# LayerNorm row sums: from f32 matmuls on x to bf16 matmuls on a copy written by ScalarE

## Chip, cores and metric

The kernel runs on the 8 cores of one Trainium2 chip, with the same program and different data on each core. The metric is the device time of the slowest core in microseconds (us).

## What is computed

One "macaron" layer on x of shape 2 x 4096 x 2048 in f32: half a feed-forward block, attention, half a feed-forward block, each on a LayerNorm of x.

```python
def _layernorm(x, axis=-1, eps=1e-5):
    m = jnp.mean(x, axis=axis, keepdims=True)
    v = jnp.var(x, axis=axis, keepdims=True)
    return (x - m) / jnp.sqrt(v + eps)
...
    x = x + 0.5 * _L0_ffn_ref(_layernorm(x, axis=-1), L0_ffn_U, L0_ffn_V, L0_ffn_W1, L0_ffn_b1, L0_ffn_W2, L0_ffn_b2)
    x = x + _L0_attn_ref(_layernorm(x, axis=-1), L0_attn_Wq, L0_attn_Wk, L0_attn_Wv, L0_attn_q_to_latent, L0_attn_v_up, L0_attn_Wo)
    x = x + 0.5 * _L0_ffn_ref(_layernorm(x, axis=-1), L0_ffn_U, L0_ffn_V, L0_ffn_W1, L0_ffn_b1, L0_ffn_W2, L0_ffn_b2)
```

The feed-forward block is a mixture over 8 low-rank maps (V, then U) with weights softmax(relu(x W1) W2). The attention is causal with 16 heads and 64-wide latent keys and values.

## The kernel before

Each core owns 1024 tokens of one sequence, but computes keys and values for all 4096 of it, in four blocks of 1024 tokens. The activations lie transposed: `x_res` is 128 partitions x 16 chunks x 1024 tokens in f32, where chunk c holds features 128c to 128c+127. A sum over the features of a token is therefore a sum over partitions and chunks, and TensorE makes it with a column of ones as weights, accumulating over the chunks in PSUM.

For each of the four blocks (loop `for j in range(4)`, from line 754) the order is:

1. Four loads of `x_res` (L762), issued by the sync engine. From the second block on, each waits until the previous block's second LayerNorm has read its chunks.
2. `emit_ln` (LN1) writes the scaled activations to `xhat` in bf16.
3. `emit_ffn`: the dense projection with W1 (`emit_big_proj`, L320), the mixture weights, the product with V (L517), their gate, replicated by two small matmuls for each of four parts (L547) and multiplied in by VectorE (L557), the product with U (L575), and the addition to `x_res` on VectorE (L585).
4. `emit_ln` again (LN2), into the same `xhat`.
5. The key/value projection (L787), which reads `xhat`; VectorE copies the result out (L805), and its TensorE token is `kv_tok`.

Behind the fourth block come the query projection, the attention, the output projection (additions to `x_res` in L1563), a ninth `emit_ln` into `xhat3`, a last feed-forward block and the store.

So `emit_ln` runs nine times. In it, a sum stage loops over the 16 chunks. ScalarE (ACT) squares the chunk into the bf16 buffer `ln_sq` (L178). TensorE makes four matmuls of 512 columns: two f32 ones straight from `x_res` into `ln_sum` (L185, L188), then, after waiting for the square, two bf16 ones from the square into `ln_sq` in PSUM (L192, L194). There is one square buffer (the list of two names the same one twice), so ACT waits with each square for TensorE's last matmul of the chunk before. Then VectorE and ACT work out mean and reciprocal deviation (L201 to L226), TensorE replicates it over the partitions (L232, L234), and VectorE multiplies all 16 chunks into `dst` (L244), which is `xhat`.

At the end of `emit_ln` and of `emit_ffn` a `load_fence` makes TensorE and ACT wait for VectorE's last product or addition, so that neither starts the next stage early. `wait0` hands `emit_ln` one token for each chunk: a load's in LN1, an addition's in the others. All order between engines is in semaphores written by hand: `ct` counts TensorE, `cs` ACT, `cv` VectorE.

Of the kernel before, what the change touches and what calls it, by code (L numbers as in the profile page):

```python
# [12 lines left out]
AF = mybir.ActivationFunctionType  # L13
# [5 lines left out]
NTOK = 1024  # L19
# [11 lines left out]
def uid():  # L31
    _UID[0] += 1
    return _UID[0]
# [102 lines left out]
def load_fence(block, engines, sem, val):  # L136
    for name in engines:
        @getattr(block, name)
        def _(e):
            e.wait_ge(sem, val)  # L140
# [12 lines left out]
def emit_ln(nc, block, bufs, S, src_chunks, dst, wait0=None, mrr=None):  # L153
    w0 = wait0 if isinstance(wait0, list) else \
        ([wait0] + [None] * (NCH - 1) if wait0 is not None else [None] * NCH)
    ct, cs, cv = S['ct'], S['cs'], S['cv']
    onesb = bufs['ones_bf']
    u = uid()
    with contextlib.ExitStack() as ps:
        p_sum = ps.enter_context(nc.psum_tensor(f"ln_sum{u}", [1, NTOK], F32))  # L160
        p_sq = ps.enter_context(nc.psum_tensor(f"ln_sq{u}", [1, NTOK], F32))
        p_rrep = ps.enter_context(nc.psum_tensor(f"ln_rrep{u}", [128, NTOK], F32))
        sq2 = [ps.enter_context(nc.sbuf_tensor(f"ln_sq2_{u}0", [128, NTOK],
                                               BF16))] * 2
        m_sb = ps.enter_context(nc.sbuf_tensor(f"ln_m{u}", [1, NTOK], F32))
        t2 = ps.enter_context(nc.sbuf_tensor(f"ln_t2{u}", [1, NTOK], F32))
        rstd = ps.enter_context(nc.sbuf_tensor(f"ln_r{u}", [1, NTOK], F32))
        sq_toks = []
        mm_toks = []
        for c in range(NCH):  # L170
            par = c % 2
            @block.scalar
            def _(s, c=c, par=par):
                if w0[c] is not None:
                    s.wait_ge(w0[c][0], w0[c][1])
                if c >= 1:
                    s.wait_ge(ct.h, mm_toks[c - 1])
                s.activation(sq2[par][:, :], src_chunks[c],  # L178
                             AF.Square).then_inc(cs.h, 1)
            sq_toks.append(cs.inc())  # L180
            @block.tensor
            def _(t, c=c, par=par):
                if w0[c] is not None:
                    t.wait_ge(w0[c][0], w0[c][1])
                t.matmul(p_sum[:, 0:512], bufs['ones_f'][:, 0:1],  # L185
                         src_chunks[c][:, 0:512],
                         start=(c == 0), stop=(c == NCH - 1))
                t.matmul(p_sum[:, 512:1024], bufs['ones_f'][:, 0:1],  # L188
                         src_chunks[c][:, 512:1024],
                         start=(c == 0), stop=(c == NCH - 1))  # L190
                t.wait_ge(cs.h, sq_toks[c])
                t.matmul(p_sq[:, 0:512], onesb[:, 0:1], sq2[par][:, 0:512],  # L192
                         start=(c == 0), stop=(c == NCH - 1))
                t.matmul(p_sq[:, 512:1024], onesb[:, 0:1],  # L194
                         sq2[par][:, 512:1024],
                         start=(c == 0), stop=(c == NCH - 1)).then_inc(ct.h, 1)
            mm_toks.append(ct.inc())
        @block.vector
        def _(v):
            v.wait_ge(ct.h, mm_toks[-1])  # L200
            v.tensor_scalar(m_sb[:, :], p_sum[:, :], 1.0 / E,  # L201
                            None, ALU.mult).then_inc(cv.h, 1)
            v.wait_ge(cv.h, cv.n + 1)
            v.tensor_tensor(t2[:, :], m_sb[:, :], m_sb[:, :],
                            ALU.mult).then_inc(cv.h, 1)
            v.wait_ge(cv.h, cv.n + 2)
            v.tensor_scalar(t2[:, :], t2[:, :], EPS, None,
                            ALU.subtract).then_inc(cv.h, 1)
            v.wait_ge(cv.h, cv.n + 3)
            v.scalar_tensor_tensor(t2[:, :], p_sq[:, :], 1.0 / E, t2[:, :],  # L210
                                   ALU.mult, ALU.subtract).then_inc(cv.h, 1)
        cv.inc(3)
        var_tok = cv.inc()
        @block.scalar
        def _(s):
            s.wait_ge(cv.h, var_tok)
            s.activation(rstd[:, :], t2[:, :], AF.Ln).then_inc(cs.h, 1)
            s.wait_ge(cs.h, cs.n + 1)
            s.activation(t2[:, :], rstd[:, :], AF.Exp,
                         scale=-0.5).then_inc(cs.h, 1)  # L220
        cs.inc(1)
        rstd_tok = cs.inc()
        @block.vector
        def _(v):
            v.wait_ge(cs.h, rstd_tok)
            v.scalar_tensor_tensor(mrr[:, :], m_sb[:, :], -1.0, t2[:, :],  # L226
                                   ALU.mult, ALU.mult).then_inc(cv.h, 1)
        mr_tok = cv.inc()
        @block.tensor
        def _(t):  # L230
            t.wait_ge(cs.h, rstd_tok)
            t.matmul(p_rrep[:, 0:512], bufs['onesr_f'][:, :], t2[:, 0:512],  # L232
                     start=True, stop=True)
            t.matmul(p_rrep[:, 512:1024], bufs['onesr_f'][:, :],  # L234
                     t2[:, 512:1024], start=True, stop=True).then_inc(ct.h, 1)
        rep_tok = ct.inc()
        last = None
        apply_toks = []
        for c in range(NCH):
            @block.vector  # L240
            def _(v, c=c):
                if c == 0:
                    v.wait_ge(ct.h, rep_tok)
                v.tensor_mul(dst[:, NTOK * c:NTOK * (c + 1)], src_chunks[c],  # L244
                             p_rrep[:, :]).then_inc(cv.h, 1)
            last = cv.inc()
            apply_toks.append(last)
        load_fence(block, ('tensor', 'scalar'), cv.h, last)
        return last, apply_toks, mr_tok
# [342 lines left out]
def alloc_common(nc, e):  # L592
    b = {}
    b['w2_sb'] = e(nc.sbuf_tensor("w2_sb", [128, NCH * 8], BF16))
    b['b1_sb'] = e(nc.sbuf_tensor("b1_sb", [128, NCH], F32))
    b['b2_sb'] = e(nc.sbuf_tensor("b2_sb", [8, 1], F32))
    b['repsel_sb'] = e(nc.sbuf_tensor("repsel_sb", [8, 4 * 128], BF16))
    b['ident_f'] = e(nc.sbuf_tensor("ident_f", [128, 128], F32))
    b['ident_bf'] = e(nc.sbuf_tensor("ident_bf", [128, 128], BF16))
    b['ones_f'] = e(nc.sbuf_tensor("ones_f", [128, 1], F32))  # L600
    b['ones_bf'] = e(nc.sbuf_tensor("ones_bf", [128, 1], BF16))
    b['onesr_f'] = e(nc.sbuf_tensor("onesr_f", [1, 128], F32))
    b['onesr_bf'] = e(nc.sbuf_tensor("onesr_bf", [1, 128], BF16))
    b['consts'] = e(nc.sbuf_tensor("consts_sb", [1, 2], F32))
    return b
# [33 lines left out]
def build_fused():  # L639
# [38 lines left out]
    with contextlib.ExitStack() as stx:  # L678
# [5 lines left out]
        bufs = alloc_common(nc, e)  # L684
# [6 lines left out]
        ct, cs, cv = S['ct'], S['cs'], S['cv']  # L691
# [7 lines left out]
        with contextlib.ExitStack() as ph1:  # L699
# [50 lines left out]
            for j in range(4):  # L750
                xq_toks = []
                for qd in range(4):
# [5 lines left out]
                    def _(sy, j=j, qd=qd, rel=rel, dxn=dx.n):  # L758
                        sy.wait_ge(dx.h, dxn)
                        if rel is not None:  # L760
# [5 lines left out]
                    xq_toks.append(dx.inc(16))  # L766
                w0 = [(dx.h, xq_toks[c // 4]) for c in range(NCH)]
                _, ln1_ap, mr1 = emit_ln(nc, block, bufs, S, x_chunks, xhat,
                                         wait0=w0, mrr=mrr1)
                res_toks = emit_ffn(nc, block, bufs, S, x_chunks, xhat,  # L770
# [3 lines left out]
                                    first=(j == 0), zps=kv_ps)  # L774
                w2l = [(cv.h, res_toks[c]) for c in range(NCH)]
                _, ln2_q, mr2 = emit_ln(nc, block, bufs, S, x_chunks, xhat,
                                        wait0=w2l, mrr=mrr2)
                if True:
# [21 lines left out]
                    kv_tok = ct.inc()  # L800
# [9 lines left out]
                def _(g, j=j, kvs_tok=kvs_tok):  # L810
# [3 lines left out]
                    g.dma_start(out=vt512[:, :, 128 * j:128 * j + 128],  # L814
                                in_=kv512[64:128, :, :]).then_inc(dlat.h, 16)
                dlat.inc(32)

            def qt_cb(m, pap, mm_tok):
                @block.vector
                def _(v, m=m, pap=pap, mm_tok=mm_tok):  # L820
                    v.wait_ge(ct.h, mm_tok)
                    v.tensor_copy(bbuf[:, NTOK * m:NTOK * (m + 1)],
                                  pap[:, :]).then_inc(cv.h, 1)
                return (cv.h, cv.inc())
# [720 lines left out]
        with contextlib.ExitStack() as f2:  # L1545
# [13 lines left out]
            def wo_cb(m, pap, mm_tok):  # L1559
# [12 lines left out]
            zps2 = f2.enter_context(  # L1572
                nc.psum_tensor("zps2", [128, NTOK], F32))
            _, ln3_ap, mr3 = emit_ln(
                nc, block, bufs, S, x_chunks, xhat3,
                wait0=[(cv.h, wo_toks[c]) for c in range(NCH)], mrr=mrr3)
# [98 lines left out]
```

## Time and profile before

| | |
|---|---|
| median of 3 runs | 3349.59 us (3349.21 to 3351.09) |
| the profiled execution | 3348.29 us |
| its span, slowest core (core 4) | 3346.8 us |
| spans of all cores | 3331.1 to 3346.8 us |
| mean granted TensorE clock | 0.743 to 0.745 on all cores |
| busy shares | TensorE 73%, VectorE 37%, ScalarE 27%, GpSimd 2% |

Times in the trace count from the start of core 4's span. A row of the timeline is one instruction or a few of a kind in a row: start, duration, engine and line; the brackets give how long the engine stood idle before it and what released it. PE is TensorE, PEld its weight loads, DVE VectorE, ACT ScalarE. A matmul's recorded duration holds its way through the array, so that records overlap: the distance between starts is what it costs in a stream. The granted clock is 1.00 at 2.4 GHz and 0.50 at 1.2 GHz.

### The profile page before, as it was taken

The page shows a single profiled execution, that of the slowest core. Times are in us where ns is not written, and L with a number is a line of the kernel's source. Part 1 is how long each engine was busy: PE and PEld are TensorE (multiplying, and loading weights), DVE is VectorE, ACT ScalarE, POOL GpSimd, SP SyncE. Part 2 cuts the span into 40 slices and gives each one's busy share as a digit, 9 for nine tenths or more (in the row PEclk, how much of TensorE's full clock was granted, in tenths as well). Part 3 has the DMA queues.
Part 4 walks back from the last instruction along what each step waited for, and adds up shares of the span by engine and source line. Part 5 has one row for each costly group of instructions (what it writes and reads, how often), then busy time and mean ns, then how long its engine had stood idle before and what let it go on. Part 6 is the DMA issues. An engine that isn't in the chain of part 4 may idle for free.

```text
span 3346.8 us, 29415 instructions; the slowest of 8 cores (3331.1 to 3346.8 us)
## 1 busy us (share of the span) xinstructions
PE 2435.8 (73%) x8607; PEld 859.8 (26%) x8607; DVE 1253.7 (37%) x2561; ACT 888.4 (27%) x1917; POOL 52.2 (2%) x78
## 2 busy tenths in 40 slices
PE   5988669866987599849456666666666656498897
PEld 1333124312432143214111111111111111142333
DVE  2003220332014300331256666666666666412103
ACT  2110211022102210200035545555455454302110
POOL 0000000000000000000100000000000000000000
PEclk8999889888988799969655555555555555599998
DMA  4330233123410432032100000000000000130332
GB/s 127 68 65 0 104 63 63 26 76 79 69 32 11 125 69 51 0 53 51 31 1 1 1 1 1 1 1 1 1 1 1 1 1 1 31 70 10 67 75 101
DMA packets 15266, 128.00 MB, mean 38 GB/s; under 512 B 6433, under 2 KB 6746, under 8 KB 7626
## 3 DMA queue, kind: packets, MB, share of 16 engines
q0 software_dynamic: 6864, 82.28, 13.8%
q1 hardware_dynamic: 8250, 43.83, 3.7%
q8 instruction: 78, 1.28, 0.2%
q14 instruction: 74, 0.61, 0.1%
HBM read 196.53 MB, written 9.27 MB: 61 GB/s over the span
## 4 chain that ended last, share of the span: by engine, by line
PE 59%; DVE 18%; ACT 11%; issue 7%; DMA 3%; DVEq 1%; ACTq 0%; POOL 0%; SPq 0%; POOLq 0%
PE bp_p L320 24%; DVE xhat L244 5%; PE PC L1468 5%; PE fe_p L575 4%; PE fe_p L517 4%; DVE madd L1395 4%; PE ln_sum L185 4%; PE ln_sum L188 4%; ACT madd L1387 3%; ACT probs L1423 3%; PE PA L1303 2%; PE bp_p L333 2%; PE bp_cs L290 1%; ACT probs L1416 1%; PE kv_ps L787 1%
## 5 line engine op out<-in xcount | busy, mean ns | idle before, releaser
L320 PE MATMUL bp_p<-xhat,wslotP 128*128 128x512 bf16 x2560 | 574.5, 383 | 56.3 <-DVE xhat L244 56.3
L1468 PE MATMUL PC<-qlat_h,kaug 65*128 65x512 bf16 (+3 forms) x768 | 340.9, 506 | 200.5 <-ACT probs L1423 191.0
L1447 PE MATMUL CV<-probs,vtT 128*65 128x512 bf16 (+3 forms) x768 | 345.8, 519 | 150.0 <-ACT probs L1423 150.0
L178 ACT ACTIVATE ln_sq<-x_res 128x1024 bf16<-128x1024 f32 x144 | 152.1, 1056 | 724.8 <-DVE x_res L585 317.9
L320 PEld LDWEIGHTS bp_p<-xhat,wslotP 128*128 128x128 bf16 x2560 | 246.0, 99 | 383.0 <-issue 104.4
L1395 DVE TENSOR_TENSOR madd<-madd,mr 128x256 f32<-128x256 f32 (+1 forms) x512 | 209.2, 409 | 263.8 <-ACT madd L1387 159.0
L1387 ACT ACTIVATE madd<-PC 128x256 f32<-128x256 f32 (+1 forms) x512 | 185.0, 361 | 353.5 <-PE PC L1468 350.6
L360 ACT ACTIVATE bbuf<-bp_p,b_sb 128x1024 bf16<-128x1024 f32 x80 | 89.1, 1113 | 674.1 <-PE bp_p L333 674.1
L1423 ACT ACTIVATE probs<-madd 128x256 bf16<-128x256 f32 (+1 forms) x512 | 206.4, 403 | 224.4 <-DVE madd L1395 221.3
L1373 DVE COPY_PREDICATED mr<-bandm_sb,ob 128x256 bf16<-128x256 uint8 (+1 forms) x512 | 210.4, 411 | 54.6 <-DVE ob L1359 2.3
L1416 ACT ACTIVATE probs<-PC 128x512 bf16<-128x512 f32 (+3 forms) x512 | 213.7, 446 | 0.0
L1447 PEld LDWEIGHTS CV<-probs,vtT 128*65 128x65 bf16 x768 | 111.5, 153 | 385.0 <-issue 375.6
L1468 PEld LDWEIGHTS PC<-qlat_h,kaug 65*128 65x128 bf16 x768 | 81.3, 109 | 373.5 <-issue 365.1
L244 DVE TENSOR_TENSOR xhat<-x_res,ln_rrep 128x1024 bf16<-128x1024 f32 x144 | 163.7, 1211 | 24.1 <-PE ln_rrep L234 24.1
L414 DVE TENSOR_SCALAR ffn_zsb<-kv_ps,b_sb 8x1024 f32<-8x1024 f32 x4 | 5.1, 1272 | 440.0 <-PE kv_ps L404 440.0
L185 PE MATMUL ln_sum<-x_res,ones_f 128*1 128x512 f32 x288 | 148.7, 598 | 17.8 <-DMA x_res<-xall 9.9
L188 PE MATMUL ln_sum<-x_res,ones_f 128*1 128x512 f32 x288 | 147.9, 595 | 0.0
L1359 DVE TENSOR_SCALAR ob<-qshrepb,ksumT 128x256 bf16<-128x256 bf16 (+1 forms) x512 | 140.6, 275 | 0.0
L201 DVE TENSOR_SCALAR ln_m<-ln_sum 1x1024 f32<-1x1024 f32 x9 | 10.9, 1212 | 321.0 <-PE ln_sq L194 321.0
L1303 PE MATMUL PA<-rcp_row,onesr_f 1*128 1x512 f32 x64 | 65.3, 1120 | 89.1 <-ACT rcp_row L1290 89.1
L320 PE MATMUL bp_p<-bbuf,wslotF 128*128 128x512 bf16 x512 | 113.3, 385 | 18.5 <-DMA wslotF<-woq 18.5
L575 PE MATMUL fe_p<-ffn_vx,wslotP 128*128 128x512 bf16 x512 | 120.2, 400 | 6.6 <-DVE ffn_vx L557 6.6
(170 smaller groups left out, 2010.2 us busy)
## 6 DMA issues: line engine op xcount, KB each, us to landing
x_res<-xall SPq DMA_DIRECT2D x16, 2048.0 KB, 8.8
wslotP<-w1q POOLq DMA_DIRECT2D x16, 2048.0 KB, 16.7
wslotP<-varr POOLq DMA_DIRECT2D x4, 2048.0 KB, 15.6
wslotP<-uarr POOLq DMA_DIRECT2D x4, 2048.0 KB, 15.8
wslotP<-wqq POOLq DMA_DIRECT2D x4, 2048.0 KB, 15.5
wslotF<-woq POOLq DMA_DIRECT2D x4, 2048.0 KB, 15.5
wslotF<-w1q POOLq DMA_DIRECT2D x4, 2048.0 KB, 14.9
yout<-x_res SPq DMA_DIRECT2D x4, 2048.0 KB
```

What stands on the lines that cost most here:

```text
L185: t.matmul(p_sum[:, 0:512], bufs['ones_f'][:, 0:1], src_chunks[c][:, 0:512], start=(c == 0), stop=(c == NCH - 1))
L188: t.matmul(p_sum[:, 512:1024], bufs['ones_f'][:, 0:1], src_chunks[c][:, 512:1024], start=(c == 0), stop=(c == NCH - 1))
L244: v.tensor_mul(dst[:, NTOK * c:NTOK * (c + 1)], src_chunks[c], p_rrep[:, :]).then_inc(cv.h, 1)
L320: mi = t.matmul(P[par][:, 512 * half:512 * half + 512], lhsT, rhs_sb[:, NTOK * k + 512 * half: NTOK * k + 512 * half + 512], start=(k == 0 ...
L575: mi = t.matmul(P[par][:, 512 * half:512 * half + 512], lhsT, vx[:, NTOK * j + 512 * half: NTOK * j + 512 * half + 512], start=(j == 0), s ...
L1373: v.copy_predicated(mr_sb[r][:, 0:lead], bandm_sb[:, 256 * r:256 * r + lead], ob_sb[i % 2][:, 0:lead]).then_inc(cv.h, 1)
L1387: s.activation(madd2_sb[i % 2][:, 0:lead], PC[:, qlo + dlt:qlo + dlt + lead], AF.Copy).then_inc(cs.h, 1)
L1395: v.tensor_tensor(madd2_sb[i % 2][:, 0:lead], madd2_sb[i % 2][:, 0:lead], mr_sb[i % 4][:, 0:lead], ALU.add).then_inc(cv.h, 1)
L1416: s.activation(probs[i % 2][:, a:b], PC[:, a + dlt:b + dlt], AF.Exp).then_inc(cs.h, 1)
L1423: s.activation(probs[i % 2][:, qlo:qlo + lead], madd2_sb[i % 2][:, 0:lead], AF.Exp).then_inc(cs.h, 1)
L1447: mi = t.matmul(CV[0:65, a:b], vtT[:, 66 * j:66 * j + 65], probs[j % 2][:, a:b], start=(j == 0), stop=last)
L1468: mi = t.matmul(PC[:, a + dlt:b + dlt], kaug[0:65, 128 * i:128 * i + 128], ql[0:65, a:b], start=True, stop=True)
```

## The change

In each chunk ACT first copies the f32 chunk into its place in `dst` as bf16, and then squares it as before. TensorE waits for both, and then sums the bf16 copy with bf16 ones instead of the f32 chunk with f32 ones. The later product (L244) overwrites the copy. Each copy carries the same waits as the square: the chunk's own token, and TensorE's last matmul of the chunk before. As the copy writes `xhat` earlier than the product did, LN1 of the blocks 2 to 4 (and the ninth LayerNorm, which pops the entry that the fourth block left) also waits for the key/value projection to have read it.

```diff
@@ -167,6 +167,7 @@
         rstd = ps.enter_context(nc.sbuf_tensor(f"ln_r{u}", [1, NTOK], F32))
         sq_toks = []
         mm_toks = []
+        dst_free = bufs.pop('ln_dst_free', None)
         for c in range(NCH):
             par = c % 2
             @block.scalar
@@ -175,20 +176,27 @@
                     s.wait_ge(w0[c][0], w0[c][1])
                 if c >= 1:
                     s.wait_ge(ct.h, mm_toks[c - 1])
+                if dst_free is not None:
+                    s.wait_ge(dst_free[0], dst_free[1])
+                s.activation(dst[:, NTOK * c:NTOK * (c + 1)], src_chunks[c],
+                             AF.Copy).then_inc(cs.h, 1)
+                if w0[c] is not None:
+                    s.wait_ge(w0[c][0], w0[c][1])
+                if c >= 1:
+                    s.wait_ge(ct.h, mm_toks[c - 1])
                 s.activation(sq2[par][:, :], src_chunks[c],
                              AF.Square).then_inc(cs.h, 1)
+            cs.inc(1)
             sq_toks.append(cs.inc())
             @block.tensor
             def _(t, c=c, par=par):
-                if w0[c] is not None:
-                    t.wait_ge(w0[c][0], w0[c][1])
-                t.matmul(p_sum[:, 0:512], bufs['ones_f'][:, 0:1],
-                         src_chunks[c][:, 0:512],
+                t.wait_ge(cs.h, sq_toks[c])
+                t.matmul(p_sum[:, 0:512], onesb[:, 0:1],
+                         dst[:, NTOK * c:NTOK * c + 512],
                          start=(c == 0), stop=(c == NCH - 1))
-                t.matmul(p_sum[:, 512:1024], bufs['ones_f'][:, 0:1],
-                         src_chunks[c][:, 512:1024],
+                t.matmul(p_sum[:, 512:1024], onesb[:, 0:1],
+                         dst[:, NTOK * c + 512:NTOK * (c + 1)],
                          start=(c == 0), stop=(c == NCH - 1))
-                t.wait_ge(cs.h, sq_toks[c])
                 t.matmul(p_sq[:, 0:512], onesb[:, 0:1], sq2[par][:, 0:512],
                          start=(c == 0), stop=(c == NCH - 1))
                 t.matmul(p_sq[:, 512:1024], onesb[:, 0:1],
@@ -814,6 +822,7 @@
                     g.dma_start(out=vt512[:, :, 128 * j:128 * j + 128],
                                 in_=kv512[64:128, :, :]).then_inc(dlat.h, 16)
                 dlat.inc(32)
+                bufs['ln_dst_free'] = (ct.h, kv_tok)
 
             def qt_cb(m, pap, mm_tok):
                 @block.vector
```

## Rows read from the trace of the kernel before

**Rows 1.** The page: span, TensorE's busy share, granted clock in 40 slices.

```profile
span 3346.8 us, 29415 instructions; the slowest of 8 cores (3331.1 to 3346.8 us)
...
PE 2435.8 (73%) x8607; PEld 859.8 (26%) x8607; DVE 1253.7 (37%) x2561; ACT 888.4 (27%) x1917; POOL 52.2 (2%) x78
...
PEclk8999889888988799969655555555555555599998
```

**Rows 2.** The page's costliest groups: busy us, mean ns of one, idle before.

```profile
L178 ACT ACTIVATE ln_sq<-x_res 128x1024 bf16<-128x1024 f32 x144 | 152.1, 1056 | 724.8 <-DVE x_res L585 317.9
...
L1387 ACT ACTIVATE madd<-PC 128x256 f32<-128x256 f32 (+1 forms) x512 | 185.0, 361 | 353.5 <-PE PC L1468 350.6
L360 ACT ACTIVATE bbuf<-bp_p,b_sb 128x1024 bf16<-128x1024 f32 x80 | 89.1, 1113 | 674.1 <-PE bp_p L333 674.1
...
L185 PE MATMUL ln_sum<-x_res,ones_f 128*1 128x512 f32 x288 | 148.7, 598 | 17.8 <-DMA x_res<-xall 9.9
L188 PE MATMUL ln_sum<-x_res,ones_f 128*1 128x512 f32 x288 | 147.9, 595 | 0.0
```

**Rows 3.** Windows of the nine sum stages: three kinds, and their sum.

```profile
core 4: us, PE busy (x) PEld busy (x) DVE busy (x) ACT busy (x) POOL busy (x), PEclk, DMA share, GB/s
322.30:357.00 34.70, 34.53 (x96) 7.93 (x96) 0.00 (x0) 16.88 (x16) 0.00 (x0) 1.00 0.00 0
396.20:430.70 34.50, 34.46 (x96) 7.83 (x96) 1.22 (x1) 15.84 (x15) 1.41 (x2) 1.00 0.24 85
...
23.00:60.50 37.50, 37.38 (x96) 8.25 (x96) 0.00 (x0) 16.90 (x16) 0.00 (x0) 1.00 0.47 168
sum 314.60, PE 313.60 PEld 71.44 DVE 3.67 ACT 148.87 POOL 4.23; mean PE 34.84 PEld 7.94 DVE 0.41 ACT 16.54 POOL 0.47
```

**Rows 4.** Timeline of one chunk in the first sum stage.

```profile
40.94 1.02 PE L185 MATMUL ln_sum<-x_res,ones_f 128*1 128x512 f32 x2
41.20 1.06 ACT L178 ACTIVATE ln_sq<-x_res 128x1024 bf16<-128x1024 f32 x1 [1.09 <-PE ln_sq L194]
...
41.80 1.02 PE L188 MATMUL ln_sum<-x_res,ones_f 128*1 128x512 f32 x2
...
42.66 0.38 PE L192 MATMUL ln_sq<-ln_sq,ones_bf 128*1 128x512 bf16 x1
...
42.87 0.38 PE L194 MATMUL ln_sq<-ln_sq,ones_bf 128*1 128x512 bf16 x1
...
43.09 1.02 PE L185 MATMUL ln_sum<-x_res,ones_f 128*1 128x512 f32 x2
43.35 1.06 ACT L178 ACTIVATE ln_sq<-x_res 128x1024 bf16<-128x1024 f32 x1 [1.09 <-PE ln_sq L194]
```

**Rows 5.** Timeline in the attention: two ACTIVATEs in a row, and a hand-over.

```profile
2201.49 0.42 ACT L1423 ACTIVATE probs<-madd 128x256 bf16<-128x256 f32 x1 [0.41 <-DVE madd L1395]
...
2201.81 0.37 ACT L1387 ACTIVATE madd<-PC 128x256 f32<-128x256 f32 x1
...
2202.05 0.61 PE L1447 MATMUL CV<-probs,vtT 128*65 128x512 bf16 x1 [0.77 <-ACT probs L1423]
```

**Rows 6.** Timeline at the start of the first sum stage, at the lower clock.

```profile
26.42 0.63 PE L192 MATMUL ln_sq<-ln_sq,ones_bf 128*1 128x512 bf16 x1
...
26.85 0.63 PE L194 MATMUL ln_sq<-ln_sq,ones_bf 128*1 128x512 bf16 x1
```

**Rows 7.** Timeline of the gate replication (L547), TensorE alone.

```profile
281.58 0.59 PE L547 MATMUL fe_p<-ffn_a8s,repsel_sb 8*128 8x512 bf16 x2 [1.48 <-DVE ffn_vx L533]
283.71 0.59 PE L547 MATMUL fe_p<-ffn_a8s,repsel_sb 8*128 8x512 bf16 x2 [1.54 <-DVE ffn_vx L557]
285.84 1.01 PE L547 MATMUL fe_p<-ffn_a8s,repsel_sb 8*128 8x512 bf16 x2 [1.54 <-DVE ffn_vx L557]
```

**Rows 8.** Windows in the attention and in the gate replication.

```profile
1700.00:2900.00 1200.00, 748.35 (x1878) 227.11 (x1878) 782.76 (x1995) 609.81 (x1621) 14.07 (x14) 0.50 0.00 1
281.60:284.50 2.90, 1.16 (x4) 0.20 (x4) 1.24 (x2) 0.00 (x0) 0.00 (x0) 1.00 0.00 0
284.90:291.00 6.10, 2.01 (x4) 0.26 (x4) 3.24 (x3) 0.00 (x0) 0.00 (x0) 0.50 0.00 0
```

## The prediction

> **What bounds the kernel now.** I read the page first: the span, the engine shares and the slices of granted clock [rows 1]. TensorE is busy 73% of the span, and the slices show stretches near full clock broken by lower ones, and one long stretch near half clock, the attention. Then the costliest groups [rows 2]. The change touches nine LayerNorm sum stages of 16 chunks each (two per column block for four blocks, and one behind the output projection), so 144 chunks; the f32 sums (L185 and L188, 288 records each) hold TensorE for 148.7 + 147.9 us.
>
> Then a table of those nine stages [rows 3]. In each one TensorE is busy from edge to edge (34.53 of 34.70 us, 34.46 of 34.50 us), the granted clock is 1.00, and ACT is busy about half of it (16.88 us). The first stage takes 37.38 us because it starts at the lower clock. So here TensorE is the bound, and ACT's square is cover.
>
> The timeline of one chunk says why [rows 4]. From one ACTIVATE to the next is 43.35 - 41.20 = 2.15 us. TensorE's records start at 40.94, 41.80, 42.66, 42.87 and again 43.09: each of the two f32 sums holds it for 0.86 us, in two records, and each of the two bf16 sums of squares for 0.215 us; 2 x 0.86 + 2 x 0.215 = 2.15. ACT squares for 1.06 us and then waits 1.09 us for TensorE. The square of chunk c starts 0.10 us after TensorE's last matmul of chunk c-1 ends (42.87 + 0.38 = 43.25, and 43.35), but the f32 sums of chunk c do not need the square, so they run beside it. That overlap is the point of the whole argument.
>
> **The change, part by part.**
>
> *TensorE.* The f32 sums become bf16: two records of 0.43 us turn into one of 0.215 us. Per chunk TensorE's work falls from 2.15 to 4 x 0.215 = 0.86 us at the full clock.
>
> *ACT.* Each chunk gets a second ACTIVATE of the same size (f32 to bf16, 128x1024), which I price as the square, 1056 ns [rows 2]. As the other end I take 1113 ns, the costliest ACTIVATE with the same output size in the page's groups [rows 2]: 0.06 us per chunk, +8 us in all. No table reload is to be expected: Copy already runs in the attention (L1387) between Exp instructions. Two ACTIVATEs in a row overlap a little: one that starts at 2201.49 and lasts 0.42 is followed at 2201.81, 0.10 us before its end, although a semaphore wait stands between them too [rows 5]. So the pair takes 1.06 - 0.10 + 1.06 = 2.01 us. The bound on the other side is no overlap and a gap of 0.10 us, as behind a wait that really blocks: 2.21 us.
>
> *The order.* This is what counts. TensorE now waits for the copy and the square before its first matmul of the chunk, and the copy waits for TensorE's last matmul of the chunk before, though it writes another part of xhat each time and has no need to. Nothing of the two engines overlaps any more, and the loop is a plain chain: pair on ACT, hand-over, four matmuls, hand-over. ACT to TensorE takes 0.14 us (2201.49 + 0.42 = 2201.91, matmul at 2202.05 [rows 5]); TensorE to ACT 0.10 us as above. The four matmuls take three spacings and one full length: 3 x 0.215 + 0.38 = 1.03 us at the full clock [rows 4], 3 x 0.43 + 0.63 = 1.92 us at the lower one [rows 6].
>
> Period of a chunk: at the full clock 2.01 + 0.14 + 1.03 + 0.10 = 3.28 us; at the lower clock 2.01 + 0.14 + 1.92 + 0.10 = 4.17 us. Either is more than 2.15. Queued behind the waits is only this stage itself: on ACT the next chunk's pair, on TensorE the next chunk's matmuls; the end of the stage is what VectorE's statistics wait for, and from there to the next stage the chain is what it was. Slower chunks only hide the x loads better.
>
> *Which clock.* TensorE would be idle 2.25 us of every 3.28 us. The nearest place in the trace is the gate-replication step (L547): two 512-column matmuls, then a wait for VectorE [rows 7, 8]. The first two pairs are at the full clock, 2.13 us apart (0.59 us each); by the third pair the records are 1.01 us long and the granted clock is 0.50, that is 1.2 GHz. Before the fall, matmuls 0.215 us apart filled 0.43 of each 2.13 us, or 20%; the recorded busy share was 1.16 of 2.90 us, 40%. Here it would be 0.86 of 3.28 us, 26%, and recorded 31%. By the columns it is a little more than in L547, by the recorded share a little less: I take the two as equally thin. Would it come back up? At 4.17 us TensorE is busy 1.92, or 46%. In the attention it is busy 748 of 1200 us, 62%, at a granted clock of 0.50 throughout [rows 8]. So I take the lower clock, from the first or second chunk of each stage on.
>
> *The added wait for kv_tok.* In blocks 2 to 4 the first stage's copy may not overwrite xhat until the key/value projection has read it. TensorE runs the projection and the old sums without a break; now TensorE idles while ACT does its first pair. The stage thus starts for ACT 0.10 us after the projection's end. The wait is repeated before each of the 16 copies, and behind the last projection too, but from the second chunk on it is long satisfied: nothing, hidden behind the wait for TensorE; if each repeat cost 0.05 us (about half of a hand-over [rows 4]), 64 of them are 3 us.
>
> **The sum.** A stage from ACT's first start to TensorE's last end is 16 x 4.17 - 0.10 = 66.6 us. Four second stages and the last one were 34.53 + 0.10 = 34.63 us: +32.0 each, 160. Three first stages of blocks 2 to 4 were 34.46 us and become 66.7: +32.2 each, 97. The very first was 37.4 and becomes 66.6: +29. Together +286 us. Off that come chunks that still run at the full clock, 4.17 - 3.28 = 0.89 us each: I take one and a half in each of the three stages that follow the projection directly, and half a one in the five that follow VectorE's last residual addition, 7 in all: -6 us. So +280 us. The profiled execution took 3348.3 us (its span 3346.8 and 1.5 around it), which makes 3628 us; the median of the runs is 1.3 us above the profiled one, well inside the rounding.
>
> Around that: no overlap within the pair is 144 x 0.20 = +29 us (3657), the dearer copy +8, four chunks at the full clock in each of nine stages instead of seven in all about -26 us (3602). Own range of this case: 3595 to 3662.
>
> **The rivals.**
>
> 1. *The clock stays up.* The period is 3.28 us, a stage 52.4 us: 5 x 17.8 + 3 x 18.0 + 16 = +159 us, 3507 us. For it: the stages before hold 1.00 with only one output column in use, and the thin activity is only slightly thicker than in L547. Against it: the fall in L547 by the third pair [rows 7, 8]. Chance 0.08.
> The Trainium skill ("TensorE: Matmul & The Clock Gate", section "Why this matters for your kernels") ties a fall in mid-kernel to one idle gap, and the one it names is longer than any this loop leaves; by it the clock would stay up and the time be this rival's 3507 us. Here the trace speaks against it: in L547 the idle gaps were 1.5 us and the clock fell.
>
> 2. *The clock swings.* It falls, comes back and falls; halfway between the two sums, 3348 + (280 + 159) / 2 = 3567 us. For it: nothing in the nine stages. Against: 1200 us of attention at 0.50 and no return. Chance 0.04.
> The same page's section "A second HAM failure mode: psum-queue depth-cycling" describes such a swing where groups of matmuls are parted by short idle times; by it the sum would be this rival's 3567 us, and no row here shows it lasting.
>
> 3. *Faster.* ACT runs ahead of TensorE, as it would if each wait of the copy were already met when it is reached. Then ACT alone sets the period, two ACTIVATEs at 0.95 us from start to start, 1.90 us, and the time is 3348 - 144 x 0.25 = 3312 us. It decides only if pair, matmuls and hand-overs together come under 2.15 us, so with a pair under 2.15 - 1.03 - 0.24 = 0.88 us, less than one ACTIVATE. In the diff both waits for TensorE's token stand before each ACTIVATE, and the page's square does wait 1.09 us there. Chance 0.02.
>
> 4. *No change*: the bf16 matmuls or the copies prove free because the stages are not on the chain after all. Against: TensorE fills each stage and VectorE waits for it. Chance 0.01.
>
> **How the numbers follow.** Forecast case 0.85, rivals 0.08, 0.04, 0.02 and 0.01. The predicted time is the forecast's, 3628 us. The range 3588 to 3662 holds nearly all of its own case and leaves out the rest, somewhat under 2 in 10. A measurement of this kernel tells about 0.2% from no change; slower by more than that is 0.97, within 0.01, faster 0.02.
>
> **What would show it.** In the new profile: ACT's groups in emit_ln twice 144 records of 1056 ns, back to back in pairs, each pair behind a wait for TensorE of some 2 us; TensorE's records for the row sums at half their number and about 0.6 us long; the granted clock near 0.5 in all nine stages; the first block's second stage some 67 us long. ACT waiting about 1.2 us instead, with records of 0.38 us, would be rival 1. I would be wrong by a large amount if the clock answers otherwise than in L547, and by a small one if the pair doesn't overlap. The time between stages should not move; if the dense projections behind them came up to full clock later than before, my sum would be too low.

## The result, and the profile after

The changed kernel takes 3627.8 us (median of 10 runs) where the kernel before takes 3350.3 us: a ratio of 1.083 (95% interval 1.0815 to 1.0839), forecast 3628 us. The profiled execution took 3626.2 us, 277.9 us more than the one before. Times of the runs below are those of the profiled execution; where one die ran at a lower clock than the other in some executions, ratios rest on the rest, and in the run with the copy on VectorE, whose profiled execution (3242.3 us) was slowed on one die, so does the time, and its views are from core 5 of the other die.

The page of the changed kernel (span, engine shares, granted clock in 40 slices), and its groups for the sum stage with the columns of [rows 2]:

```profile
span 3624.6 us, 29182 instructions; the slowest of 8 cores (3611.8 to 3624.6 us)
...
PE 2386.6 (66%) x8319; PEld 840.6 (23%) x8319; DVE 1253.7 (35%) x2561; ACT 1024.4 (28%) x2061; POOL 52.3 (1%) x78
...
PEclk9998559965698558975985555555555555596798
...
L181 ACT ACTIVATE xhat<-x_res 128x1024 bf16<-128x1024 f32 x144 | 152.1, 1056 | 858.2 <-DVE x_res L593 320.4
...
L194 PE MATMUL ln_sum<-xhat,ones_bf 128*1 128x512 bf16 x144 | 83.4, 579 | 343.1 <-ACT ln_sq L187 343.1
...
L187 ACT ACTIVATE ln_sq<-x_res 128x1024 bf16<-128x1024 f32 x144 | 149.6, 1039 | 0.0
```

TensorE has less to do (2386.6 us busy where [rows 1] have 2435.8) in a longer span, ACT 136 us more. The row for L194 has the finding in one place: before 144 matmuls TensorE stood idle for 343.1 us in all, released each time by the square. [rows 2] have 17.8 us there, most of it behind a load.

The nine sum stages as windows on core 5, the slowest of this execution, against [rows 3] (columns as there; five of nine shown, and the sum):

```profile
22.50:86.90 64.40, 28.62 (x62) 5.72 (x63) 0.00 (x0) 32.02 (x32) 0.00 (x0) 1.00 0.26 98
352.10:415.80 63.70, 27.84 (x62) 5.64 (x63) 0.00 (x0) 32.03 (x32) 0.00 (x0) 0.53 0.00 0
456.60:522.20 65.60, 28.68 (x62) 5.76 (x63) 1.22 (x1) 32.03 (x32) 1.41 (x2) 0.51 0.12 36
768.10:832.60 64.50, 28.64 (x62) 5.72 (x63) 0.00 (x0) 32.03 (x32) 0.00 (x0) 0.51 0.00 0
873.20:938.00 64.80, 27.84 (x62) 5.67 (x63) 1.22 (x1) 32.03 (x32) 1.40 (x2) 0.54 0.12 37
...
sum 581.60, PE 255.28 PEld 51.35 DVE 3.67 ACT 288.24 POOL 4.22; mean PE 28.36 PEld 5.71 DVE 0.41 ACT 32.03 POOL 0.47
```

581.6 us where they were 314.6: 267 us of the 278. Each window stops two matmuls short (62 of 64), some 1.1 us before the stage's end, which is the rest. TensorE is busy 28 us of each 64, ACT 32 us, and neither while the other is: 28.4 + 32.0 = 60 of 64.6 us, and the rest is hand-overs. The granted clock is 0.51 to 0.54. (For the first stage the column says 1.00; the last section comes to that.)

One chunk of the second stage in the timeline, at the lower clock:

```profile
356.40 1.04 ACT L187 ACTIVATE ln_sq<-x_res 128x1024 bf16<-128x1024 f32 x1
...
357.58 0.59 PE L194 MATMUL ln_sum<-xhat,ones_bf 128*1 128x512 bf16 x1 [2.24 <-ACT ln_sq L187]
...
357.96 0.63 PE L197 MATMUL ln_sum<-xhat,ones_bf 128*1 128x512 bf16 x1
...
358.39 0.63 PE L200 MATMUL ln_sq<-ln_sq,ones_bf 128*1 128x512 bf16 x1
...
358.82 0.63 PE L202 MATMUL ln_sq<-ln_sq,ones_bf 128*1 128x512 bf16 x1
359.55 1.06 ACT L181 ACTIVATE xhat<-x_res 128x1024 bf16<-128x1024 f32 x1 [2.11 <-PE ln_sq L202]
```

Read it as a chain: the square ends at 357.44, TensorE starts 0.14 us later, its last matmul ends at 359.45, the next copy starts 0.10 us later. Nothing lies beside anything. [rows 4] had the f32 sums beside the square. The first chunk of this stage was still at 2.4 GHz (its four matmuls took 0.38 us each); the one shown is the second, and it was not.

### The profile page after: what moved, and what is told of

It is laid out like the page before. It is cut to its first block, busy times and chain, and to the rows that moved or that the text cites. A ratio compares the mean times of both kernels' runs of the same rounds, so it can differ in the third digit from the quotient of the medians.

```text
span 3624.6 us, 29182 instructions; the slowest of 8 cores (3611.8 to 3624.6 us)
## 1 busy us (share of the span) xinstructions
PE 2386.6 (66%) x8319; PEld 840.6 (23%) x8319; DVE 1253.7 (35%) x2561; ACT 1024.4 (28%) x2061; POOL 52.3 (1%) x78
## 4 chain that ended last, share of the span: by engine, by line
PE 53%; DVE 17%; ACT 14%; issue 11%; DMA 4%; DVEq 1%; ACTq 1%; POOL 0%; SPq 0%; POOLq 0%
PE bp_p L328 22%; DVE xhat L252 5%; PE PC L1477 4%; PE fe_p L583 4%; PE fe_p L525 4%; ACT ln_sq L187 4%; DVE madd L1404 4%; ACT madd L1396 3%; ACT probs L1432 2%; PE ln_sum L194 2%; PE PA L1312 2%; PE ln_sq L202 2%; PE ln_sq L200 2%; PE ln_sum L197 2%; PE bp_p L341 1%
## 5 line engine op out<-in xcount | busy, mean ns | idle before, releaser
L181 ACT ACTIVATE xhat<-x_res 128x1024 bf16<-128x1024 f32 x144 | 152.1, 1056 | 858.2 <-DVE x_res L593 320.4
L194 PE MATMUL ln_sum<-xhat,ones_bf 128*1 128x512 bf16 x144 | 83.4, 579 | 343.1 <-ACT ln_sq L187 343.1
```

Of the source, the lines that this page charges most:

```text
L194: t.matmul(p_sum[:, 0:512], onesb[:, 0:1], dst[:, NTOK * c:NTOK * c + 512], start=(c == 0), stop=(c == NCH - 1))
```

## The experiments

Theory A, the prediction's: the change takes the overlap of the two engines away, so that a chunk costs the sum of its parts, and with that little work TensorE's clock falls. Theory B: what costs is ACT's second instruction per chunk. Theory C: the order and the copy are harmless and only the clock is at fault. The first diff is against the kernel before, the others against the changed one.

### One wait moved in the kernel before

```diff
-                if w0[c] is not None:
-                    t.wait_ge(w0[c][0], w0[c][1])
+                t.wait_ge(cs.h, sq_toks[c])
                 t.matmul(p_sum[:, 0:512], bufs['ones_f'][:, 0:1],
...
-                t.wait_ge(cs.h, sq_toks[c])
                 t.matmul(p_sq[:, 0:512], onesb[:, 0:1], sq2[par][:, 0:512],
```

> The kernel before, with one wait moved: TensorE waits for the square before its f32 sums too. No copy, no bf16 sums. Theory A (the order is what costs: ACT and TensorE no longer overlap): the period of a chunk is the square 1.06 + hand-over 0.15 + four matmuls 2 x 0.86 + 0.215 + 0.38 = 2.32 + hand-over 0.10 = 3.63 us where it was 2.15; nine stages of 16 chunks make about +208 us, 3556 us, if the clock stays at 1.00 with TensorE busy 64% of the period. If the clock falls: 1.06 + 0.15 + 4.47 + 0.10 = 5.78 us, about 3865 us. Theory B (what costs is the second ACTIVATE per chunk, not the order): no added ACT work here, so 3348 us.

Measured: 3555.1 us, ratio 1.062 (1.0588 to 1.065). The second stage as a window, and TensorE's and ACT's rows of one chunk from the timeline:

```profile
345.00:401.00 56.00, 35.25 (x92) 6.87 (x93) 0.00 (x0) 16.91 (x16) 0.00 (x0) 1.00 0.00 0
```

```profile
355.89 1.06 ACT L178 ACTIVATE ln_sq<-x_res 128x1024 bf16<-128x1024 f32 x1 [2.55 <-PE ln_sq L192]
357.10 1.02 PE L184 MATMUL ln_sum<-x_res,ones_f 128*1 128x512 f32 x2 [1.30 <-ACT ln_sq L178]
...
359.03 0.38 PE L192 MATMUL ln_sq<-ln_sq,ones_bf 128*1 128x512 bf16 x1
359.50 1.06 ACT L178 ACTIVATE ln_sq<-x_res 128x1024 bf16<-128x1024 f32 x1 [2.55 <-PE ln_sq L192]
```

The period is 3.61 us, the clock stays at 1.00, TensorE does the same work as before (35.25 us) and is idle 1.30 us in each chunk. Theory B is out as the whole story: with no instruction added anywhere, a wait in another place costs 207 us (3555.1 - 3348.3). As to the clock: with TensorE busy 63% of the window it stays up.

### The copy alone

The changed kernel, but TensorE sums the f32 chunk as before, ahead of its wait; the copy is made and feeds nothing.

```diff
+                if w0[c] is not None:
+                    t.wait_ge(w0[c][0], w0[c][1])
+                t.matmul(p_sum[:, 0:512], bufs['ones_f'][:, 0:1],
+                         src_chunks[c][:, 0:512],
...
                 t.wait_ge(cs.h, sq_toks[c])
-                t.matmul(p_sum[:, 0:512], onesb[:, 0:1],
-                         dst[:, NTOK * c:NTOK * c + 512],
...
```

> The changed kernel's copy on ACT is kept, with all its waits, but TensorE sums the f32 chunk as before, ahead of its wait for the square; the copy feeds nothing. Theory A: the f32 sums (1.72 us) lie beside the pair of ACTIVATEs (2.00 us); the period is 2.00 + 0.15 + 0.215 + 0.38 + 0.10 = 2.85 us, about +98 us over the kernel before, 3447 us, clock 1.00. Theory B: the second ACTIVATE is the whole cost, so about 3626 us, as the changed kernel.

Measured: 3445.9 us, 97.7 us above the profiled execution of the kernel before. Timeline of one chunk:

```profile
342.49 1.04 ACT L187 ACTIVATE ln_sq<-x_res 128x1024 bf16<-128x1024 f32 x1
...
343.68 0.38 PE L202 MATMUL ln_sq<-ln_sq,ones_bf 128*1 128x512 bf16 x1 [0.53 <-ACT ln_sq L187]
...
343.89 0.38 PE L204 MATMUL ln_sq<-ln_sq,ones_bf 128*1 128x512 bf16 x1
...
344.11 1.02 PE L195 MATMUL ln_sum<-x_res,ones_f 128*1 128x512 f32 x2
344.37 1.06 ACT L181 ACTIVATE xhat<-x_res 128x1024 bf16<-128x1024 f32 x1 [0.83 <-PE ln_sq L204]
```

A period of 2.84 us, clock 1.00. The second ACTIVATE costs about 98 us as long as the f32 sums lie beside it: the pair, 2.00 us, has outgrown their 1.72. The other 180 us of the change are the order and the clock.

### The clock held up by filler

In each chunk 32 small matmuls with thrown-away results on TensorE, ahead of its wait.

```diff
+                for _f in range(32):
+                    t.matmul(p_rrep[0:1, 128 * (_f % 4):128 * (_f % 4) + 128],
+                             onesb[:, 0:1], bufs['w2_sb'][:, 0:128],
+                             start=True, stop=True)
                 t.wait_ge(cs.h, sq_toks[c])
```

> The changed kernel with 32 matmuls of 128 columns (one output column, results thrown away) on TensorE before its wait in each chunk, where it is idle for 2.24 us; at 2.4 GHz they fit (about 1.7 us), at 1.2 GHz they take 3.4 us and lengthen the first chunks. Theory A with the lower clock as a second part: the clock stays at 1.00, the period falls from 4.11 to 2.00 + 0.15 + 1.00 + 0.10 = 3.25 us, 144 x 0.86 = -123 us, 3503 us. Theory C (the lower clock is all that is wrong with the change): at or under 3350 us. If the fillers don't lift the clock, slower than 3626 us, near 3850.

Measured: 3507.4 us, ratio 1.048 (1.0446 to 1.0506). The second stage as a window:

```profile
338.20:391.00 52.80, 45.10 (x576) 33.86 (x576) 0.44 (x1) 32.10 (x32) 0.00 (x0) 1.00 0.01 2
```

One chunk of it in the timeline (L194 is the filler here):

```profile
351.05 1.95 PE L194 MATMUL ln_rrep<-w_sb,ones_bf 128*1 128x128 bf16 x32
...
352.27 1.04 ACT L187 ACTIVATE ln_sq<-x_res 128x1024 bf16<-128x1024 f32 x1
...
353.46 0.38 PE L198 MATMUL ln_sum<-xhat,ones_bf 128*1 128x512 bf16 x1 [0.46 <-ACT ln_sq L187]
...
354.58 1.06 ACT L181 ACTIVATE xhat<-x_res 128x1024 bf16<-128x1024 f32 x1 [1.26 <-PE ln_sq L206]
```

Adding 4608 useless matmuls makes the kernel 119 us faster than the change (3626.2 - 3507.4). The clock is at 1.00 in the stage and the period is 3.27 us (3.33 in four of the nine). The fillers are over at 353.00, before the square ends at 353.31, so the chain is the change's own. So the lower clock is worth 119 us, and theory C is out: with the clock up the change still costs 159 us (3507.4 - 3348.3).

### The copy freed from a wait that it never needed

```diff
-                if c >= 1:
-                    s.wait_ge(ct.h, mm_toks[c - 1])
-                if dst_free is not None:
+                if c == 0 and dst_free is not None:
                     s.wait_ge(dst_free[0], dst_free[1])
                 s.activation(dst[:, NTOK * c:NTOK * (c + 1)], src_chunks[c],
                              AF.Copy).then_inc(cs.h, 1)
```

> The changed kernel, but the copy no longer waits for TensorE's last matmul of the chunk before (it never needed to), and waits for the key/value projection in the first chunk alone; the square waits as before, with its one buffer. Theory A: the copy goes into ACT's idle time, the period is the square 1.04 + 0.15 + 1.86 + 0.10 = 3.15 us at the lower clock, a stage 4.1 + 15 x 3.15 = 51.4 us, about 3496 us; if the clock stays up, 2.29 us and 3372 us. Theory B: the same ACTIVATEs, so 3626 us as the changed kernel.

Measured: 3499.6 us, 126.6 us less than the changed kernel's profiled execution; the ratio to the kernel before is 1.051 with a wide interval (1.0371 to 1.0658). Windows at the start of the second stage and in its steady part, then the timeline:

```profile
338.30:343.00 4.70, 1.22 (x5) 0.39 (x6) 0.00 (x0) 4.34 (x5) 0.00 (x0) 0.87 0.00 0
345.00:389.00 44.00, 26.08 (x56) 5.11 (x56) 0.00 (x0) 26.84 (x27) 0.00 (x0) 0.50 0.00 1
```

```profile
344.04 0.63 PE L200 MATMUL ln_sq<-ln_sq,ones_bf 128*1 128x512 bf16 x1
344.77 1.06 ACT L185 ACTIVATE ln_sq<-x_res 128x1024 bf16<-128x1024 f32 x1 [1.16 <-PE ln_sq L200]
345.73 1.04 ACT L179 ACTIVATE xhat<-x_res 128x1024 bf16<-128x1024 f32 x1
```

The period is 3.16 us as worked out; the copy now runs beside TensorE. The clock falls in this version too and stays down, with TensorE busy 59% of the steady window.

### No wait for TensorE at all

The copy as in the last run, and a place of its own for each square in `bbuf` (`bufs['hbuf']` in the code), idle in these stages, so that the square doesn't wait either.

```diff
-                if w0[c] is not None:
-                    s.wait_ge(w0[c][0], w0[c][1])
-                if c >= 1:
-                    s.wait_ge(ct.h, mm_toks[c - 1])
-                s.activation(sq2[par][:, :], src_chunks[c],
-                             AF.Square).then_inc(cs.h, 1)
+                s.activation(bufs['hbuf'][:, NTOK * c:NTOK * (c + 1)],
+                             src_chunks[c], AF.Square).then_inc(cs.h, 1)
```

> The changed kernel with ACT freed of every wait for TensorE in the sum stage: the copy waits for its chunk alone (and once for the key/value projection), the square goes to a place of its own for each chunk in bbuf, which is idle in these stages. Theory A (the order): ACT sets the pace with two ACTIVATEs at 0.96 us from start to start, 1.92 us a chunk; TensorE's four matmuls fit beside them at either clock (0.86 or 1.71 us). A stage is 16 x 1.92 + 0.1 + 0.15 + 1.86 = 32.8 us where the kernel before has 34.6, about -15 us in all (the first stage waits for its last load): 3335 us, a little faster than the kernel before. Theory B (the second ACTIVATE costs what the change cost): 3626 us.

Measured: 3323.4 us, ratio 0.991 (0.9883 to 0.9936). It still has the copy on ACT and the bf16 sums, all the work of the change, and it is 303 us faster than the change and 25 us faster than the kernel before. Windows of the third stage, the first chunks, the next, and the steady part:

```profile
390.40:394.50 4.10, 1.02 (x4) 0.30 (x5) 1.23 (x1) 4.03 (x5) 1.41 (x2) 1.00 0.54 128
394.90:398.00 3.10, 2.70 (x7) 0.49 (x5) 0.00 (x0) 3.10 (x4) 0.00 (x0) 0.50 0.98 354
402.00:421.00 19.00, 10.23 (x40) 2.80 (x41) 0.00 (x0) 18.87 (x20) 0.00 (x0) 1.00 0.00 0
```

ACT is busy 18.87 of 19.00 us: it is the bound, at 1.90 us a chunk. In this stage the clock falls once, and at that pace TensorE, at 1.2 GHz, is busy 2.70 of 3.10 us; then it is back at 1.00. I had said 3335 us: the pair is 1.90 and not 1.92 us, and the stage ends at the upper clock and not the lower.

### The copy on VectorE

As the last run, but the copy is VectorE's.

```diff
+            @block.vector
+            def _(v, c=c):
+                if w0[c] is not None:
+                    v.wait_ge(w0[c][0], w0[c][1])
+                if c == 0 and dst_free is not None:
+                    v.wait_ge(dst_free[0], dst_free[1])
+                v.tensor_copy(dst[:, NTOK * c:NTOK * (c + 1)],
+                              src_chunks[c]).then_inc(cv.h, 1)
+            cp_toks.append(cv.inc())
...
+                t.wait_ge(cv.h, cp_toks[c])
                 t.wait_ge(cs.h, sq_toks[c])
```

> As the run with ACT freed, but VectorE, idle in this stage, makes the bf16 copies beside ACT's squares. Theory A: the period is the longest of ACT 0.96 us, VectorE's copy (not measured yet; taken as 1.1 us) and TensorE's 0.86 us at 2.4 GHz or 1.71 us at 1.2 GHz. TensorE would be busy about 80% of the period at 2.4 GHz, and the clock should stay up: a stage of some 19 us where it was 34.6, with loads bounding the very first, -130 us in all, 3220 us. If the clock falls: 28.5 us a stage, about 3298 us. Theory C (no gain can be had from bf16 sums here): 3350 us.

Measured: 3208.5 us (the median), ratio 0.957 (0.955 to 0.9594). The second stage on core 5 as a window, and from the timeline VectorE's sixteen copies:

```profile
312.30:329.10 16.80, 15.22 (x64) 4.46 (x64) 9.78 (x17) 15.25 (x16) 0.00 (x0) 1.00 0.00 1
```

```profile
312.36 9.72 DVE L187 CAST xhat<-x_res 128x1024 bf16<-128x1024 f32 x16
```

The stage takes 16.8 us where [rows 3] have 34.7. The copy costs VectorE 9.72 / 16 = 0.61 us, little more than half of the 1.1 I had assumed, so that ACT's squares set the pace at 0.95 us and TensorE is busy 91% of the window at 2.4 GHz. In the first stage of each block loads now hold the engines up as well, as ACT's rows of the third stage on the same core show:

```profile
358.38 7.68 ACT L178 ACTIVATE bbuf<-x_res 128x1024 bf16<-128x1024 f32 x8 [22.33 <-DVE xhat L253]
369.09 3.90 ACT L178 ACTIVATE bbuf<-x_res 128x1024 bf16<-128x1024 f32 x4 [3.03 <-DMA x_res<-xall]
379.25 3.90 ACT L178 ACTIVATE bbuf<-x_res 128x1024 bf16<-128x1024 f32 x4 [6.26 <-DMA x_res<-xall]
```

So the bf16 sums are worth some 140 us with the copy on VectorE and no wait that isn't needed.

### The repeated wait

```diff
-                if dst_free is not None:
+                if c == 0 and dst_free is not None:
                     s.wait_ge(dst_free[0], dst_free[1])
```

> The changed kernel with the wait for the key/value projection before the first chunk's copy alone, not before each. If the repeated wait, long satisfied, is what makes the period 4.16 us in the four stages that carry it and 4.11 us in the five that do not, all nine now show 4.11 us: 64 x 0.055 = 3.5 us less, about 3623 us. If it is something else about those stages (the loads that run beside them), the period there stays at 4.16 us.

Measured: 3623.8 us, 2.4 us less than the changed kernel's profiled execution, which by itself is within what this kernel's executions differ. The period decides. Two copies of the third stage, in the changed kernel and then in this one:

```profile
460.78 1.06 ACT L181 ACTIVATE xhat<-x_res 128x1024 bf16<-128x1024 f32 x1 [2.16 <-PE ln_sq L202]
...
464.95 1.06 ACT L181 ACTIVATE xhat<-x_res 128x1024 bf16<-128x1024 f32 x1 [2.16 <-PE ln_sq L202]
```

```profile
460.73 1.06 ACT L181 ACTIVATE xhat<-x_res 128x1024 bf16<-128x1024 f32 x1 [2.10 <-PE ln_sq L202]
...
464.84 1.06 ACT L181 ACTIVATE xhat<-x_res 128x1024 bf16<-128x1024 f32 x1 [2.11 <-PE ln_sq L202]
```

4.17 us before, 4.11 us here, as in all other stages; the loads that run beside this stage are the same in both, so they are not the cause. A wait that has long been met, placed behind one that blocks, costs 0.055 us.

## Why the prediction was right

The mechanism was the one forecast: the engines take turns, a chunk costs the sum of its parts, and the clock is the lower one. The runs with one wait moved, with fillers and with ACT freed bear out each part by itself.

**The period.** Forecast 4.17 us, measured 4.11 us in five stages and 4.16 us in the four with the repeated wait. By parts: the pair 2.01 us forecast, 2.00 measured (the square behind the copy starts 0.96 us after it and is recorded with 1.04 us); ACT to TensorE 0.14 us, measured 0.14 to 0.15; the four matmuls 1.92 us, measured 1.87 (359.45 - 357.58); TensorE to ACT 0.10, measured 0.10. The matmuls are shorter because the first spacing is 0.38 us and not 0.43. That no table load would come between copy and square also held: the changed kernel's trace has a single one, at its start, as the one before.

**Chunks at the full clock.** Forecast seven of 144; in the profiled core there are three that save 0.8 us each (one in the second stage and one each in the first stages of the blocks 3 and 4) and one in the ninth stage that saves 0.3. This term was -6 us and measured about -3; with the period 0.06 us too long in five stages (about 5 us) the two errors nearly cancel. On the profiled executions the forecast of +280 us stands against 277.9; that the median, 3627.8 us, meets 3628 to a microsecond is luck.

**The repeated wait.** Forecast 3 us at most, measured 64 x 0.055 = 3.5 us.

**The time between stages.** Said not to move: from one stage's end to the next one's start it moved by -1.2 to +2.2 us at single places (the first feed-forward block takes 2.2 us longer, the next ones about 1 us less), +0.3 us in all. I did not look into these.

**The ladder.** The parts in one order, from the runs: the copy beside the old sums +98 us; the sums behind the square as well, with the clock held up, +61 us (3507.4 - 3445.9); the clock +119 us (3626.2 - 3507.4). Together 278 us. In another order the parts differ: the order alone, on the old sums, was +207 us. The prediction's 280 us divides at the clock into 159 and 121; the 98 us for the copy alone were worked out only for its run.

**The rivals.** The clock that stays up: its price, 3507 us, is what the filler run measured; its condition was not met. By the Trainium skill's page "TensorE: Matmul & The Clock Gate", section "Why this matters for your kernels", the clock would have held. Here the measurement decides against it. The clean case is the fifth stage, which follows the projection directly; the second stage begins with a longer gap (3.62 us before its first matmul). The fifth stage's first two chunks in the timeline (the brackets give TensorE's idle time):

```profile
875.41 0.38 PE L194 MATMUL ln_sum<-xhat,ones_bf 128*1 128x512 bf16 x1 [2.24 <-ACT ln_sq L187]
...
878.73 0.59 PE L194 MATMUL ln_sum<-xhat,ones_bf 128*1 128x512 bf16 x1 [2.30 <-ACT ln_sq L187]
```

No gap there was longer than 2.3 us, and the second chunk's record is already the longer one of the lower clock.

The prediction's likeness to the gate replication was in one figure misread: 1.16 of 2.90 us is a window that ends with the second pair of matmuls, without the gap behind it. By the distance of the pairs the recorded share there was 0.59 of 2.13 us, 28%, not 40%. So this loop (31%) was the thicker of the two by both shares, and the step from the one to the other was a little less safe than it was made to look. The clock fell all the same.

The clock that swings: not in the changed kernel, where it stays down once it has fallen; in the run with ACT freed it falls and comes back. The faster one, ACT running ahead, is a real version of this kernel: I priced it at 3312 us, and it measures 3323.4.

## What to carry to other kernels

Before speeding up a bound engine by handing it other input, draw the wait graph of one loop turn: the old operand needed no other engine, the new one comes from ACT and is waited for together with the square, and that turned max(2.15, 1.06) into a sum of 4.1. (The row sums need only the copy; a TensorE wait for the copy alone ahead of them was not tried.) A wait copied along with an instruction should be asked what it protects: here the copy wrote a fresh place in each turn, and without its wait and with a buffer for each square the same work is 303 us faster. And work that is thinned out on TensorE can cost its clock, so the time of a lighter loop has to be worked out at both levels.

## What I had not expected

**The record of the clock at the start.** For the first sum stage the granted clock reads 1.00, in the table above and in [rows 3], while the matmuls there are 0.43 us apart and 0.63 us long throughout in the changed kernel:

```profile
24.65 0.58 PE L194 MATMUL ln_sum<-xhat,ones_bf 128*1 128x512 bf16 x1 [11.58 <-ACT ln_sq L187]
...
25.45 0.63 PE L200 MATMUL ln_sq<-ln_sq,ones_bf 128*1 128x512 bf16 x1
...
25.88 0.63 PE L202 MATMUL ln_sq<-ln_sq,ones_bf 128*1 128x512 bf16 x1
```

That is 1.2 GHz, as in the stage at 352 us, which reads 0.53. The column seems to hold 1.00 until the record's first change, so at the start of a trace the spacing of matmuls is the better witness. If so, the mean clock of 0.691 is too high as well, by an estimated 0.01 (65 us of 3625 at half the clock).

**Where the clock fell and where not.** These are single stretches of the traces, all but the last with four bf16 matmuls (0.86 us at 2.4 GHz) a chunk, and they give no limit. In the changed kernel it fell behind one chunk at the full clock, with the next 3.3 us later; in the run with the copy ahead also behind one, with the next 2.32 us later (342.81 - 340.49, second stage), and once down it stayed down with TensorE busy 59% of the steady window. In the run with ACT freed, 1.90 us a chunk, it was down for the first few microseconds of seven of the nine stages, in the third without an idle gap over 2.25 us before it, and not in the fifth and seventh; it rose where TensorE was busy 87% (2.70 of 3.10 us), and in the third stage's steady part it held at 1.00 with 54% (10.23 of 19.00 us). The wait moved in the kernel before kept it up at 63% of a window at 2.4 GHz. What decides between these cases no run here shows.
